# Key and value projection of axis 1: its second token tile moved right behind the first, in the PSUM bank of the group statistics

## The chip, the core and the metric

The kernel is one program on 1 core of a Trainium2 chip. The metric is the time of one execution on the device in microseconds (us), less is better. TensorE (PE) multiplies into PSUM; VectorE (DVE), ScalarE (ACT) and GpSimd (POOL) do the elementwise work; SyncE (SP) issues most transfers. Each engine takes its own instructions in order, and the engines meet at semaphores that the kernel sets and waits for by hand.

## What is computed

The input x is 8 images of 16 x 16 tokens with 256 channels. Two blocks follow each other, each with a residual:

```python
x = x + L0(_gn(x))      # linear attention: 16 heads of 16 channels, once along the columns, once along the rows
x = x + L1(_gn(x))      # softmax attention along rows and along columns, 256 channels, Gaussian distance term

# L0, for one axis (sequences of 16 tokens):
q, k, v = split(x @ w_qkv)
dots = einsum('bhie,bhje->bhij', q, k) * d ** (-0.5)
out = einsum('bhij,bhje->bhie', dots, v) @ w_out     # the two axes are added
# L1:
r_attn = softmax(q @ k over w - gw * dist);  c_attn = softmax(q @ k over h - gw * dist)
out = (r_attn @ v + c_attn @ v) @ Wo + bo
```

`_gn` is a group normalisation over 32 groups of 8 channels and all 256 tokens of an image. L0 has no softmax, so the kernel forms key-times-value first and multiplies the queries into it.

## The kernel before

One image is one batch step b, 0 to 7. Its 256 tokens are two token tiles of 128, its 256 channels two channel halves. Nearly every product runs as three passes (hi times hi, hi times lo, lo times hi) over operands that are split in two FP32R parts: ScalarE writes the high part from PSUM, VectorE writes the low part as the difference. All these products stand on line 995 in the helper `product`.

The order of work is written out by hand for each engine, as `attention(b)` and then `project(b)`, unrolled for b = 0, in a loop for b = 1 to 6, and with a tail of its own for b = 7. Each step works on three images at once: L0's attention of image b, L1's softmax attention of image b-1, and L0's projections of image b+1.

What matters here, by name:

- `project_kv(b+1, i)` on TensorE makes keys and values (512 columns) of tile i of the next image: i = 0 and 1 are the two token tiles of axis 1, i = 2 and 3 those of axis 0. It is 6 matmuls of 128x512 into `proj_bank[i]`. `take_kv(b+1, i)` on ScalarE (L383) copies the bank to SBUF and raises `kv_taken`.
- `place_v` on SyncE waits until both tiles of an axis are taken and issues 8 transfers (L253) that lay the values out by sequence in `v_wide`. `key_value(b+1, axis)` on TensorE (L1050) waits for them.
- `project_q(b+1, 0)` (12 matmuls of 128x256) makes the queries of axis 1, and `take_q` (L387) copies them.
- L0's output of image b: `transpose_output(b, axis)` on TensorE (L1081), `split_o(b, axis)` on ScalarE (L409, the high part `o_hi`) and on VectorE (L676, the low part `o_lo`), then `project_out(b, axis)` on TensorE (12 matmuls). Axis 1 goes first.
- L1's weights of image b-1: `exponentials` on ScalarE (L415, L417), `invert_sums` on VectorE (L715), `weights` on GpSimd (L342 to L348), then `transpose_weights` on TensorE (L1127).
- `group_mean` (L1000) and `group_variance` (L1004) average the statistics over a group in columns 0 to 3 of `bank[1]`, for both normalisations. `normalise(1, b)` on ScalarE (L375) follows from them, and after it `mask_kv` (L394) and the next step's `queries` (L1072).

TensorE's order around the change is: `transpose_output(b, 1)`, `project_kv(b+1, 0)`, `project_q(b+1, 0)`, `transpose_output(b, 0)`, `project_out(b, 1)`, `project_kv(b+1, 1)`, `project_out(b, 0)`, then in `project` `project_kv(b+1, 2)`, `transpose_weights(b-1)`, `project_kv(b+1, 3)`, `group_mean(1, b)`. ScalarE's order is: `split_o(b, 1)`, `take_kv(0)`, `take_q(0)`, `split_o(b, 0)`, `exponentials`, `take_kv(1)`, `take_kv(2)`. Tile 1 goes to `bank[2]`, which the transposed output of axis 1 holds until `o_lo` has been read.

```python
def project(b, has_prev, has_next):
    if has_next:
        take_kv(b + 1, 1)
        take_kv(b + 1, 2)
```

Of the kernel before, what the change touches and what calls it, by code (L numbers as in the profile page):

```python
# [23 lines left out]
TILES = 2 * TT  # L24
# [11 lines left out]
def tile_of(n):  # L36

    return 1 - n // TT, n % TT


def build(nc, x, w_qkv0, w_out0, w_qkv1, w_out1, wq, bq, wk, bk, wv, bv, wo, bo, sigma, out):
    with ExitStack() as ctx:
# [3 lines left out]
        def sem(name):  # L46
            return ctx.enter_context(nc.semaphore(name))
# [88 lines left out]
        bank = [ctx.enter_context(nc.psum_tensor(f"bank{i}", [P, 512], FP32)) for i in range(8)]  # L136
# [6 lines left out]
        last_s_bank, last_at_bank, last_pv_bank = [bank[3], bank[0]], [bank[2], bank[6]], [bank[1], bank[4]]  # L143
        o_last = o_even[:, :, :, :].rearrange("p h m a -> p (h m a)").rearrange("p (c n) -> p c n", c=CC)
        t_last, vp_last, at_last, y_last, x1b_last = x_in, x_res, q[:, 0, :, :], q[:, 1, :, :], k_v[:, 0, 0, :, :]
        proj_bank, q_bank = [bank[0], bank[2], bank[4], bank[5]], [bank[7], bank[7]]
        first_bank = [bank[0], bank[3]]
        fold_bank, values_fold_bank = bank[7], bank[0]
        xt_first = attn
# [29 lines left out]
        kv_proj, kv_taken = sem("kv_proj"), sem("kv_taken")  # L179
# [181 lines left out]
        def _(act):  # L361
# [17 lines left out]
            def take_kv(b, i):  # L379
                axis, t = tile_of(i)  # L380
                src = proj_bank[i]
                act.wait_ge(kv_proj, TILES * b + i + 1)
                act.activation(k_v[:, axis, t, :, :].rearrange("p i d -> p (i d)"), src[:, :], ACT.Copy).then_inc(kv_taken, 1)  # L383

            def take_q(b, i, scale=1.0):
                act.wait_ge(q_proj, 2 * b + i + 1)
                act.activation(q[:, 1 - i, :, :].rearrange("p c n -> p (c n)"), q_bank[i][:, :], ACT.Copy, scale=scale).then_inc(q_taken, 1)  # L387
# [11 lines left out]
            def take_even(b, axis):  # L399

                act.wait_ge(o_ready, 2 * b + 2 - axis)
                for r in range(HALVES):
                    src = qkv_bank[r][:, :].rearrange("p (m s a) -> p m s a", m=TT * CC, s=2)
                    act.activation(o_even[:, r, :, :], src[:, :, 0, :], ACT.Copy, scale=parity[:, 0:1]).then_inc(o_even_done, 1)  # L404
# [19 lines left out]
            def high_t(b):  # L424
                act.wait_ge(t_ready, b + 1)
                for c in range(CC):
                    last = act.activation(t_hi[:, c, :], t_bank[:, c * TOKENS:(c + 1) * TOKENS], ACT.Identity, bias=c1[:, c:c + 1])
                last.then_inc(t_hi_done, 1)

            def high_values(b, t):  # L430
                act.wait_ge(vp_ready, TT * b + t + 1)
                act.activation(vp_hi[:, t, :], vp_banks[t][:, 0:DIM], ACT.Copy).then_inc(vp_hi_done, 1)

            def attention(b, has_prev, has_next):
                take_even(b, 1)
                if has_prev:
                    high_t(b - 1)
                mask_kv(b, 0)
                if has_prev:
                    high_values(b - 1, 0)  # L440
                if has_next:
                    normalise(0, b + 1)
                if has_prev:
                    high_values(b - 1, 1)
                take_even(b, 0)
                split_o(b, 1)
                if has_next:
                    take_kv(b + 1, 0)
                    take_q(b + 1, 0)
                split_o(b, 0)  # L450
                if has_prev:
                    exponentials(b - 1, 0)
                    exponentials(b - 1, 1)

            def next_residual(b):

                act.wait_ge(x1_ready, b)
                act.wait_ge(x_turned, b)
                act.dma_start(x_res[:, :, :], x_chan[:, :, :]).then_inc(res_loaded, 16)

            def project(b, has_prev, has_next):
                if has_next:
                    take_kv(b + 1, 1)
                    take_kv(b + 1, 2)
                    next_residual(b + 1)
                if has_prev:
                    split_attn(b - 1)
                if has_next:
                    take_kv(b + 1, 3)
                if not has_prev:  # L470
                    high_fold(wvo_hi, 3, values_fold_bank)
                normalise(1, b)
                if has_next:
                    mask_kv(b + 1, 1)
                    take_q(b + 1, 1)
# [512 lines left out]
        def _(pe):  # L988
# [9 lines left out]
            def group_mean(k, b):  # L998
                pe.wait_ge(stat_in[k], 2 * b + 1)
                pe.matmul(stat_bank[:, 0:CC], group_avg[:, :], mv[k][:, :, 0], start=True, stop=True).then_inc(stat_sum[k], 1)  # L1000
# [10 lines left out]
            def project_kv(b, i):  # L1011

                axis, t = tile_of(i)
                if i == 0:
                    pe.wait_ge(xn_split[0], b)
                if i == TT:
                    pe.wait_ge(turned, b + 1)
                hi, lo = (xt_hi, xt_lo) if axis == 0 else (xn_hi[0], xn_lo[0])
                product(proj_bank[i][:, :],
                        [((hi[:, c, t * P:(t + 1) * P], lo[:, c, t * P:(t + 1) * P]),  # L1020
                          (wqkv_hi[:, axis, c, DIM:3 * DIM], wqkv_lo[:, axis, c, DIM:3 * DIM])) for c in range(CC)]
                        ).then_inc(kv_proj, 1)
# [156 lines left out]
            def attention(b, has_prev, has_next):  # L1179

                queries(b, 1)
                if has_prev:
                    pe.wait_ge(q_taken, 2 * (b + 1))
                    project_t(b - 1)
                if has_next:
                    group_mean(0, b + 1)
                key_value(b, 0)
                if has_next:
                    group_variance(0, b + 1)
                if has_prev:  # L1190
                    project_values(b - 1, 0)
                    project_values(b - 1, 1)
                else:
                    fold_row()
                queries(b, 0)
                if has_prev:
                    pe.wait_ge(vp_lo_done, TT * (b - 1) + 1)
                    scores(b - 1, 0, y_bank)
                    scores(b - 1, 1, y_bank)
                transpose_output(b, 1)  # L1200
                if has_next:
                    if not has_prev:
                        pe.wait_ge(w_split, 1)
                    project_kv(b + 1, 0)
                    if has_prev:
                        pe.wait_ge(vp_lo_done, TT * b)
                    else:
                        pe.wait_ge(bias_step, 5)
                    project_q(b + 1, 0)
                transpose_output(b, 0)  # L1210
                if has_prev:
                    pe.wait_ge(logits_done, TT * b)
                else:
                    pe.wait_ge(w_split, 3)
                    pe.wait_ge(fold_split, 1)
                project_out(b, 1)
                if has_next:
                    project_kv(b + 1, 1)
                project_out(b, 0)

            def project(b, has_prev, has_next):

                if has_next:
                    project_kv(b + 1, 2)
                if has_prev:
                    if has_next:
                        pe.wait_ge(q_taken, 2 * (b + 1) + 1)
                    transpose_weights(b - 1)
                if has_next:
                    project_kv(b + 1, 3)  # L1230
                group_mean(1, b)
                if has_prev:
                    weighted_values(b - 1, 0)
                else:
                    fold_values(0)
                group_variance(1, b)
                if has_prev:
                    weighted_values(b - 1, 1)
                else:
                    fold_values(1)  # L1240
                if has_next:
                    key_value(b + 1, 1)
                    if has_prev:
                        pe.wait_ge(out_sum, b)
                    else:
                        pe.wait_ge(q_taken, 2 * (b + 1) + 1)
                    project_q(b + 1, 1)
                if not has_prev:
                    pe.wait_ge(fold_split, 2)
                    pe.wait_ge(r_split, 2)  # L1250
# [76 lines left out]
            fold_row()  # L1327
            pe.wait_ge(w_split, 1)
            project_kv(1, 0)
            pe.wait_ge(bias_step, 5)  # L1330
            project_q(1, 0)
            transpose_output(0, 0)
            pe.wait_ge(w_split, 3)
            pe.wait_ge(fold_split, 1)
            project_out(0, 1)
            project_kv(1, 1)
            project_out(0, 0)
            project(0, False, True)
            with pe.Fori(1, BATCHES - 1) as b:
# [113 lines left out]
```

## Time and profile before

| what | value |
|---|---|
| time, median of 3 runs | 244.22 us (243.4 to 245.59) |
| the profiled execution, its own time | 244.0 us |
| its span, first to last instruction | 242.2 us |
| mean granted TensorE clock | 0.971 of full speed |
| TensorE busy | 224.0 us, 92% of the span |
| VectorE busy | 172.0 us, 71% |
| ScalarE busy | 131.5 us, 54% |
| GpSimd busy | 67.2 us, 28% |
| transfers | 13.86 MB, mean 57 GB/s |

One loop step takes about 25.7 us. Batch b stands for the step that works on L0's attention of image b: batch 3 runs from about 102.9 to 128.6 us of the span. In a timeline row the first number is the start from the beginning of the span, the second the length; the brackets at its end give the idle time of the engine before it and what ended that. Matmuls overlap each other, so the distance from start to start says what one costs, not its length.

### The profile page before, as it was taken

The page shows a single profiled execution, that of the slowest core. Times are in us where ns is not written, and L with a number is a line of the kernel's source. Part 1 is how long each engine was busy: PE and PEld are TensorE (multiplying, and loading weights), DVE is VectorE, ACT ScalarE, POOL GpSimd, SP SyncE. Part 2 cuts the span into 40 slices and gives each one's busy share as a digit, 9 for nine tenths or more (in the row PEclk, how much of TensorE's full clock was granted, in tenths as well). Part 3 has the DMA queues.
Part 4 walks back from the last instruction along what each step waited for, and adds up shares of the span by engine and source line. Part 5 has one row for each costly group of instructions (what it writes and reads, how often), then busy time and mean ns, then how long its engine had stood idle before and what let it go on. Part 6 is the DMA issues. An engine that isn't in the chain of part 4 may idle for free.

```text
span 242.2 us, 8272 instructions
## 1 busy us (share of the span) xinstructions
PE 224.0 (92%) x3216; PEld 192.6 (80%) x3216; DVE 172.0 (71%) x507; ACT 131.5 (54%) x321; POOL 67.2 (28%) x94
## 2 busy tenths in 40 slices
PE   7999999889998999999999999999999999993980
PEld 7747889688986898789888897889878988792960
DVE  5769666687757885788568866888588856687480
ACT  2435743367736665565656673777366656726240
POOL 6400160203432164216420543124421642002000
PEclk9999979999999999999999999999999999997696
DMA  6932230322021321332032203221220212011003
GB/s 215 344 55 67 52 55 6 95 46 38 0 80 46 53 43 32 83 58 43 10 93 55 43 16 92 51 43 30 81 49 0 43 56 65 14 27 19 0 3 87
DMA packets 43824, 13.86 MB, mean 57 GB/s; under 512 B 36257, under 2 KB 42401, under 8 KB 43809
## 3 DMA queue, kind: packets, MB, share of 16 engines
q1 hardware_dynamic: 41264, 9.92, 19.8%
q10 hardware_dynamic: 2544, 3.74, 4.4%
q8 instruction: 10, 0.16, 0.3%
q14 instruction: 6, 0.04, 0.1%
HBM read 5.51 MB, written 2.10 MB: 31 GB/s over the span
## 4 chain that ended last, share of the span: by engine, by line
PE 69%; SPq 9%; ACT 5%; issue 5%; DMA 4%; DVE 3%; ACTq 2%; POOL 1%; POOLq 0%; DVEq 0%
PE bank L995 39%; SPq L253 9%; PE bank L1072 8%; PE bank L1050 6%; DMA v_wide<-k_v 4%; PE bank L1081 3%; PE bank L1256 3%; ACT k_v L383 2%; PE bank L1270 1%; PE bank L1004 1%; ACTq L499 1%; ACT kv L394 1%; PE bank L1009 1%; PE bank L1424 1%; PE bank L1174 1%
## 5 line engine op out<-in xcount | busy, mean ns | idle before, releaser
L383 ACT ACTIVATE k_v<-bank 128x512 f32<-128x512 f32 x32 | 19.0, 598 | 35.4 <-PE bank L995 29.7
L308 POOL TENSOR_TENSOR rstd<-var_eps,minus_half 128x2 f32<-128x2 f32 x16 | 11.3, 705 | 92.1 <-DVE var_eps L640 92.1
L394 ACT ACTIVATE kv<-bank,head_scale 128x256 f32<-128x256 f32 x64 | 25.0, 472 | 4.6 <-PE bank L1050 4.6
L299 POOL TENSOR_TENSOR xt_lo<-xn,xn_hi 128x256 fp32r<-128x256 f32 x14 | 18.5, 1341 | 20.9 <-DVE xn_hi L649 20.9
L657 DVE TENSOR_TENSOR kv<-bank,block_mask 128x512 f32<-128x512 f32 x32 | 20.6, 684 | 3.8 <-PE bank L1050 3.8
L1072 PE MATMUL bank<-kv,q 64*32 64x128 f32 x1024 | 19.2, 281 | 3.7 <-issue 2.3
L1050 PE MATMUL bank<-v_wide,k_v 64*32 64x128 f32 x1024 | 18.4, 273 | 2.2 <-DMA v_wide<-k_v 1.0
L1072 PEld LDWEIGHTS bank<-kv,q 64*32 64x32 f32 x1024 | 15.2, 108 | 6.5 <-issue 6.5
L404 ACT ACTIVATE o_even<-bank,parity 128x256 f32<-128x256 f32 x32 | 13.3, 469 | 8.6 <-PE bank L1072 8.6
L1050 PEld LDWEIGHTS bank<-v_wide,k_v 64*32 64x32 f32 x1024 | 14.4, 105 | 4.3 <-issue 4.0
L995 PE MATMUL bank<-o_hi,wout_hi 128*128 128x256 f32 x60 | 17.5, 292 | 0.0
L676 DVE TENSOR_TENSOR o_lo<-bank,o_hi 128x256 fp32r<-128x256 f32 x30 | 13.8, 505 | 4.7 <-ACT o_hi L409 4.7
L668 DVE SCALAR_TENSOR_TENSOR o_tok<-bank,parity,o_even 128x256 f32<-128x256 f32 x32 | 14.0, 478 | 4.6 <-ACT o_even L404 4.6
L995 PE MATMUL bank<-o_hi,wout_lo 128*128 128x256 f32 x60 | 17.0, 284 | 0.0
L995 PE MATMUL bank<-o_lo,wout_hi 128*128 128x256 f32 x60 | 16.9, 282 | 0.0
L409 ACT ACTIVATE o_hi<-bank 128x256 fp32r<-128x256 f32 x30 | 12.7, 505 | 3.0 <-PE bank L1081 3.0
L375 ACT ACTIVATE xn<-x,nbias,rstd 128x256 f32<-128x256 f32 x14 | 7.7, 594 | 11.9 <-DVE nbias L645 11.9
L387 ACT ACTIVATE q<-bank 128x512 f32<-128x512 f32 x16 | 9.6, 598 | 7.9 <-PE bank L995 5.9
L342 POOL TENSOR_TENSOR attn<-exp_col,inv_sum 128x512 f32<-128x512 f32 x6 | 6.3, 1042 | 20.5 <-DVE inv_sum L715 20.5
L771 DVE TENSOR_TENSOR x<-bank,x_res 128x512 f32<-128x512 f32 x7 | 4.8, 692 | 9.9 <-PE bank L995 9.9
L995 PE MATMUL bank<-wqkv_hi,xn_hi 128*128 128x512 f32 x28 | 11.7, 418 | 0.0
L995 PEld LDWEIGHTS bank<-o_hi,wout_hi 128*128 128x128 f32 x60 | 11.3, 189 | 0.3
(233 smaller groups left out, 698.5 us busy)
## 6 DMA issues: line engine op xcount, KB each, us to landing
v_wide<-k_v SPq DMA_DIRECT2D x122, 32.0 KB, 2.0
x_blk<-in_x_dram SPq DMA_DIRECT2D x56, 32.0 KB, 1.9
x_res<-x_chan ACTq DMA_DIRECT2D x7, 256.0 KB, 2.3
out_dram<-y_blk SPq DMA_DIRECT2D x56, 32.0 KB, 1.5
wqkv_in<-in_L_conv_w_qkv_dram SPq DMA_DIRECT2D x2, 384.0 KB, 6.4
wqkv_in<-in_L_conv_w_qkv_dram ACTq DMA_DIRECT2D x2, 384.0 KB, 7.6
wl<-in_L_conv_Wq_dram SPq DMA_DIRECT2D x1, 256.0 KB, 3.5
wl<-in_L_conv_Wk_dram ACTq DMA_DIRECT2D x1, 256.0 KB, 3.9
```

The costliest lines, as they stand in the source:

```text
L253: sp.dma_start(v_wide[tokens, axis, :, s % NEAR, :], k_v[tokens, axis, :, 1, :]).then_inc(v_placed[axis], 16)
L299: pool.tensor_tensor(xt_lo[:, c, :].rearrange("p (w h) -> p w h", w=SIDE), by_axis(xn[0][:, c, :], 0), by_axis(xn_hi[0][:, c, :].bitcast(F ...
L383: act.activation(k_v[:, axis, t, :, :].rearrange("p i d -> p (i d)"), src[:, :], ACT.Copy).then_inc(kv_taken, 1)
L394: last = act.activation(kv[axis][:, 1, :, :, :, head // 2, own].rearrange("p t c s e -> p (t c s) e"), kv_bank[1][:, :].rearrange("p (a e) ...
L404: act.activation(o_even[:, r, :, :], src[:, :, 0, :], ACT.Copy, scale=parity[:, 0:1]).then_inc(o_even_done, 1)
L409: last = act.activation(by_axis(o_hi[:, axis, c, :], axis), banks[1 - axis][:, c * TOKENS:(c + 1) * TOKENS].rearrange("p (s i) -> p s i", ...
L657: last = dve.tensor_tensor(kv[axis][:, 0, :, :, :, pair, :].rearrange("p t c s e -> p (t c s) e"), kv_bank[0][:, :].rearrange("p (a e) -> ...
L668: last = dve.scalar_tensor_tensor(o_tok[:, axis, :, :].rearrange("p t (c h a) -> p (t c) h a", c=CC, h=HALVES)[:, :, r, :], src[:, :, 1, : ...
L676: last = dve.tensor_tensor(by_axis(o_lo[:, axis, c, :], axis), banks[1 - axis][:, c * TOKENS:(c + 1) * TOKENS].rearrange("p (s i) -> p s i ...
L995: last = pe.matmul(dst, a, b, start=(first and i == 0), stop=(final and i == len(passes) - 1))
L1050: last = pe.matmul(kv_bank[r][pair * PAIR:(pair + 1) * PAIR, first:first + P], k_v[rows, axis, t, 0, channels], v_wide[rows, axis, t, :, c ...
L1072: last = pe.matmul(qkv_bank[r][quad * QUAD:(quad + 1) * QUAD, to:to + 2 * FOUR], q[rows, axis, c, first:first + QUAD], kv[axis][rows, quad ...
```

## The change

The second tile of axis 1, `project_kv(b+1, 1)`, moves on TensorE from between the two `project_out` of an image to right behind `project_kv(b+1, 0)`, for b+1 = 1 to 7. ScalarE's `take_kv(b+1, 1)` moves with it, from behind the exponentials to right behind `take_kv(b+1, 0)`. The tile's bank is `bank[1]` instead of `bank[2]`. Since `group_mean(1, b)` writes into `bank[1]` too, TensorE now waits before it until tile 1 has been taken. The first image uses the same table of banks, its order is unchanged.

```diff
-        proj_bank, q_bank = [bank[0], bank[2], bank[4], bank[5]], [bank[7], bank[7]]
+        proj_bank, q_bank = [bank[0], bank[1], bank[4], bank[5]], [bank[7], bank[7]]
...
                 split_o(b, 1)
                 if has_next:
                     take_kv(b + 1, 0)
+                    take_kv(b + 1, 1)
                     take_q(b + 1, 0)
                 split_o(b, 0)
...
             def project(b, has_prev, has_next):
                 if has_next:
-                    take_kv(b + 1, 1)
                     take_kv(b + 1, 2)
...
                     project_kv(b + 1, 0)
+                    project_kv(b + 1, 1)
                     if has_prev:
                         pe.wait_ge(vp_lo_done, TT * b)
...
                 project_out(b, 1)
-                if has_next:
-                    project_kv(b + 1, 1)
                 project_out(b, 0)
...
                 if has_next:
                     project_kv(b + 1, 3)
+                    pe.wait_ge(kv_taken, TILES * (b + 1) + 2)
                 group_mean(1, b)
...
             project_kv(1, 0)
+            project_kv(1, 1)
...
             project_out(0, 1)
-            project_kv(1, 1)
             project_out(0, 0)
```

On TensorE, in the loop step, the stretch from the last pass of `project_out(b, 1)` stands like this before (`wqkv` rows are the key and value projection, `wout` rows the output projection, `o_lo_done` says that VectorE has written the low part):

```order
L995 MATMUL bank<-o_hi,wout_lo 128x256
L995 MATMUL bank<-wqkv_hi,xn_hi 128x512
L995 MATMUL bank<-wqkv_lo,xn_hi 128x512
L995 MATMUL bank<-wqkv_hi,xn_lo 128x512
L995 MATMUL bank<-wqkv_hi,xn_hi 128x512
L995 MATMUL bank<-wqkv_lo,xn_hi 128x512
L995 MATMUL bank<-wqkv_hi,xn_lo 128x512
L995 MATMUL bank<-o_hi,wout_hi 128x256 [waits o_lo_done]
```

The six passes of the projection stand between the two output projections. After the change the same place on TensorE, from the middle of `project_out(b, 1)`, reads:

```order
L995 MATMUL bank<-o_hi,wout_hi 128x256
L995 MATMUL bank<-o_lo,wout_hi 128x256
L995 MATMUL bank<-o_hi,wout_lo 128x256
L995 MATMUL bank<-o_hi,wout_hi 128x256 [waits o_lo_done]
L995 MATMUL bank<-o_lo,wout_hi 128x256
L995 MATMUL bank<-o_hi,wout_lo 128x256
```

The row that waits for `o_lo_done` now comes right behind the last pass of `project_out(b, 1)`; the six passes stand ahead of the queries' projection.

On ScalarE, in the loop step, the row order from the axis-1 split to the next image's tiles is before (`o_hi` the high part of the output, 128x16x16 that of axis 0; `k_v` the taken keys and values):

```order
L409 ACTIVATE o_hi<-bank 128x256
L382 ISA
L383 ACTIVATE k_v<-bank 128x512 [waits kv_proj]
L386 ISA
L387 ACTIVATE q<-bank 128x512 [waits q_proj]
L409 ACTIVATE o_hi<-bank 128x16x16 [waits ot_ready]
L409 ACTIVATE o_hi<-bank 128x16x16
L415 ACTIVATE exp_row,exp_sum<-log_row,neg_max 128x128 [waits max_ready]
L417 ACTIVATE exp_col,exp_sum<-log_col,neg_max 128x256
L415 ACTIVATE exp_row,exp_sum<-log_row,neg_max 128x128 [waits max_ready]
L417 ACTIVATE exp_col,exp_sum<-log_col,neg_max 128x256
L382 REGISTER_ALU
```

After it, the same place of ScalarE reads:

```order
L409 ACTIVATE o_hi<-bank 128x256
L382 ISA
L383 ACTIVATE k_v<-bank 128x512 [waits kv_proj]
L382 REGISTER_ALU
L383 ACTIVATE k_v<-bank 128x512 [waits kv_proj]
L386 ISA
L387 ACTIVATE q<-bank 128x512 [waits q_proj]
L409 ACTIVATE o_hi<-bank 128x16x16 [waits ot_ready]
L409 ACTIVATE o_hi<-bank 128x16x16
L415 ACTIVATE exp_row,exp_sum<-log_row,neg_max 128x128 [waits max_ready]
L417 ACTIVATE exp_col,exp_sum<-log_col,neg_max 128x256
```

The second `k_v` row has moved ahead of the queries, of the axis-0 split and of the exponentials. VectorE's and GpSimd's orders are the same in both kernels.

## Rows read from the trace of the kernel before

**Rows 1.** The page: busy share of each engine, and the chain's shares by engine

```profile
PE 224.0 (92%) x3216; PEld 192.6 (80%) x3216; DVE 172.0 (71%) x507; ACT 131.5 (54%) x321; POOL 67.2 (28%) x94
...
PE 69%; SPq 9%; ACT 5%; issue 5%; DMA 4%; DVE 3%; ACTq 2%; POOL 1%; POOLq 0%; DVEq 0%
```

**Rows 2.** Chain of work that ended last, batch 3: start us, us, engine line

```profile
118.26 0.61 ACT k_v L383
118.88 0.61 SPq L253
...
123.36 1.99 DMA v_wide<-k_v
```

**Rows 3.** Waits of TensorE over the span: us in total, times, longest

```profile
PE bank L1050 <- DMA v_wide<-k_v: 1.0, 3, 0.7
```

**Rows 4.** Timeline of TensorE, batch 3: start us, us, engine line op tiles [idle before]

```profile
116.66 0.40 PE L995 MATMUL bank<-wqkv_hi,xn_hi 128*128 128x512 f32 x1
...
118.06 0.28 PE L995 MATMUL bank<-o_hi,wout_hi 128*128 128x256 f32 x1
...
120.66 0.40 PE L995 MATMUL bank<-wqkv_hi,xt_lo 128*128 128x512 f32 x1
121.11 0.63 PE L1127 MATMUL bank<-ident,attn 128*128 128x128 f32 x4
```

**Rows 5.** Timeline of ScalarE, the same stretch

```profile
114.98 0.60 ACT L387 ACTIVATE q<-bank 128x512 f32<-128x512 f32 x1 [0.84 <-PE bank L995]
115.47 1.06 ACT L409 ACTIVATE o_hi<-bank 128x256 fp32r<-128x256 f32 x2
116.32 0.38 ACT L415 ACTIVATE exp_row<-log_row,neg_max 128x128 f32<-128x128 f32 x1
...
117.95 0.20 ACT L417 ACTIVATION_READ_ACCUMULATOR exp_col<-log_col,neg_max 128x1 f32 x1
```

**Rows 6.** Timeline of VectorE, the same stretch

```profile
116.56 1.13 DVE L676 TENSOR_TENSOR o_lo<-bank,o_hi 128x256 fp32r<-128x256 f32 x2 [0.65 <-ACT o_hi L409]
118.18 0.18 DVE L715 RECIPROCAL inv_sum<-exp_sum 128x4 f32<-128x4 f32 x1 [0.49 <-ACT exp_col L417]
```

**Rows 7.** Timeline of GpSimd, the same stretch

```profile
120.13 0.88 POOL L348 TENSOR_TENSOR attn<-row_weights,attn 128x128 f32<-128x128 f32 x2
```

**Rows 8.** Timeline of TensorE, the end of batch 3

```profile
124.08 0.38 PE L1004 MATMUL bank<-shift,group_avg 128*128 128x2 f32 x2
...
125.49 1.15 PE L1050 MATMUL bank<-v_wide,k_v 64*32 64x128 f32 x64 [0.20 <-DMA v_wide<-k_v]
...
128.56 1.15 PE L1072 MATMUL bank<-kv,q 64*32 64x128 f32 x64 [0.31 <-issue]
```

**Rows 9.** Timeline of ScalarE, the end of batch 3

```profile
125.68 1.09 ACT L375 ACTIVATE xn<-x,nbias,rstd 128x256 f32<-128x256 f32 x2 [1.91 <-DVE nbias L645]
126.69 1.57 ACT L394 ACTIVATE kv<-bank,head_scale 128x256 f32<-128x256 f32 x4
```

**Rows 10.** Timeline of TensorE, the end of batch 1

```profile
72.08 0.38 PE L1004 MATMUL bank<-shift,group_avg 128*128 128x2 f32 x2
...
73.96 1.15 PE L1050 MATMUL bank<-v_wide,k_v 64*32 64x128 f32 x64 [0.68 <-DMA v_wide<-k_v]
...
77.13 1.13 PE L1072 MATMUL bank<-kv,q 64*32 64x128 f32 x63 [0.40 <-issue]
```

**Rows 11.** Timeline of VectorE, batch 0

```profile
38.70 1.11 DVE L676 TENSOR_TENSOR o_lo<-bank,o_hi 128x256 fp32r<-128x256 f32 x2 [0.81 <-ACT o_hi L409]
```

**Rows 12.** Timeline of TensorE, batch 0

```profile
40.09 0.28 PE L995 MATMUL bank<-o_hi,wout_hi 128*128 128x256 f32 x1
```

**Rows 13.** Stretches: A:B, length, busy us of each engine, granted clock, DMA share, GB/s

```profile
30.00:33.00 3.00, 3.00 (x70) 2.62 (x71) 1.66 (x4) 1.70 (x5) 1.55 (x2) 0.51 0.33 54
...
210.00:220.00 10.00, 7.96 (x113) 6.96 (x112) 8.59 (x26) 5.18 (x17) 1.04 (x1) 1.00 0.16 28
220.00:228.00 8.00, 5.83 (x27) 5.29 (x27) 4.26 (x15) 2.88 (x6) 0.74 (x1) 0.58 0.00 0
```

## The prediction

> **What bounds the kernel now.** I read the page first. TensorE is busy for 92% of the span and holds 69% of the chain that ended last; SyncE's queue and the transfers hold 13% more [rows 1]. So either more work or more waiting on TensorE shows in the time, unless it falls where TensorE already waits.
>
> Then the chain in order of time. In batch 3 it leaves TensorE at the copy of tile 1 (118.26 us), runs through SyncE's 8 issues of `v_wide` and the landing of the last (123.36 + 1.99 = 125.35), and comes back into TensorE at `key_value(b+1, 1)` [rows 2], which sat idle for 0.20 us for it [rows 8]. This is where an earlier tile 1 could help. The list of waits says how little TensorE pays there: 1.0 us in three waits over the whole span [rows 3].
>
> Last I read the stretch around the moved tile on all four engines. Two chains run beside TensorE there, and both start when `project_q(b+1, 0)` ends, because ScalarE takes the queries first and everything else behind them:
> - queries taken at 114.98, `o_hi` of axis 0 from 115.47 to 116.53 [rows 5], `o_lo` from 116.56 to 117.69 [rows 6], then TensorE may start `project_out(b, 0)`. It did so at 118.06 [rows 4]: 0.37 us of slack.
> - the exponentials from 116.32, the last sum read out at 118.15 [rows 5], the reciprocal at 118.18 [rows 6], GpSimd's weights ready at 120.13 + 0.88 = 121.01 [rows 7], then `transpose_weights` at 121.11 [rows 4]. This chain has no slack. The last pass of the projection ahead of it started at 120.66, and such passes follow each other by 0.23 us ((118.06 - 116.66) / 6), so TensorE could have gone on at 120.89. It already waited 0.22 us for GpSimd, and started 0.10 us after the weights were ready.
>
> **What the change does to these chains.** The tile costs 118.06 - 116.66 = 1.40 us on TensorE [rows 4]. No work is added: the same 1.40 us are now spent before `project_q(b+1, 0)` instead of behind it. Both chains start at the end of `project_q`, so both start 1.40 us later, while the TensorE work that covers them, between the end of `project_q` and each waiting instruction, is 1.40 us shorter.
>
> *First wait, `project_out(b, 0)`.* ScalarE takes tile 1 in the 1.40 us in which TensorE makes the queries, and was idle for 0.84 us there [rows 5]; the copy of 0.61 us [rows 2] fits. So `take_q` starts at 114.98 + 1.40 = 116.38, `o_hi` ends at 117.93, `o_lo` at 117.69 + 1.40 = 119.09. VectorE has nothing else then: it was idle for 0.65 us before [rows 6]. TensorE, with its earlier work unchanged in sum, would be ready at 118.06. It starts at 119.09 plus about 0.1 for the semaphore (the 0.10 of the weights, above): about 119.2, a stall of 1.1 us. Queued behind it are `project_kv(b+1, 2)` and all the rest of the step, and VectorE's residual `x1` waits for it.
>
> *Second wait, `transpose_weights(b-1)`.* The weights are ready at 121.01 + 1.40 = 122.41, and TensorE can start at 122.51. From the first stall alone TensorE would be ready at 120.89 + 1.1 = 122.0. So the second wait tops the first up to the full 1.40 us: the two do not add. Since this chain had no slack before, the step becomes longer by 1.40 us behind it, whatever the first wait does.
>
> *The end of the step.* What the change frees is the idle time for `v_wide`: tile 1 is taken at about 114.94 to 115.54 instead of 118.26 to 118.87, 3.3 us earlier, so its transfers land long before `key_value(b+1, 1)`. In a common step that buys nothing. From `group_variance(1, b)` at 124.08 two paths run to the next step's queries at 128.56 [rows 8]: TensorE's own, and VectorE, GpSimd and ScalarE with `normalise(1, b)` from 125.68 and the masking of the keys and values from 126.69 to 128.26 [rows 9]. ScalarE goes from the one to the other without a pause, so an earlier `key_value` does not make the masking earlier. Gain 0 in the five steps 2 to 6. Batch 1 is the exception: `key_value` waited 0.68 us and the queries came 77.13 - 72.08 = 5.05 us after `group_variance` [rows 10], against 128.56 - 124.08 = 4.48 in batch 3 [rows 8]. That step gets 5.05 - 4.48 = 0.57, say 0.6 us back.
>
> *Batch 0* has no exponentials and no weights. Its `o_lo` ends at 38.70 + 1.11 = 39.81 [rows 11] and `project_out(0, 0)` started at 40.09 [rows 12]. With 1.40 later: 41.21 + 0.1 = 41.3, a stall of 1.2 us, and nothing behind it takes that back. Batch 7 projects no next image and has no stall of its own.
>
> *Edits that I cost at nothing.* The new wait for `kv_taken` before `group_mean(1, b)`: the copy ends near 115.5, and the mean comes behind two more projections of the step. Without this cover TensorE would wait for a copy of 0.6 us. The transfers of axis 0 now wait for the copy of tile 3 instead of following those of axis 1 on SyncE's queue; that copy moves with TensorE and is over before 124.08, and 8 issues and a landing take 125.35 - 118.88 = 6.5 us [rows 2], so until 130.6. `key_value(b+1, 0)` stands behind the next queries (128.56 + 1.15, [rows 8]) and 12 passes of 256 columns, each half of 0.23: 131.1. Close, but covered, and both ends move together. The new bank: TensorE writes it only after VectorE has read the statistics of the first normalisation, which lie a whole attention stretch back.
>
> *The sum:* batch 0 +1.2, batches 1 to 6 6 x 1.40 = +8.4, batch 1 -0.6: +9.0 us. On the profiled execution's own 244.0 us (span 242.2) that makes 253.0 us; on the median of the runs, 244.22, it would be 253.2, which is no difference.
>
> *Bounds.* The least I can make of the stalls is that GpSimd's chain somehow tightens by 0.3 us per step and only the first wait counts: 1.2 + 6 x 1.1 - 0.6 = 7.2. The most, without the gain in batch 1 and with 0.1 us more per step: 1.2 + 9.0 = 10.2. On top comes the tail. TensorE's clock fell there after a stretch with 7.96 us of work in 10, and ran at 0.58 of full speed on the mean from 220 to 228 us [rows 13]. That costs up to 0.42 x 5.8 = 2.4 us, and where exactly the clock falls may shift now that the tail comes 9 us later: about 1 us either way. So 250.5 to 255.5.
>
> *The clock in the loop.* What the rows show: the granted clock held 1.00 over a stretch with 2.04 us idle in 10, and it fell to 0.51, which is the lower level of 1.2 GHz, from 30 to 33 us, and to 0.58 on the mean from 220 to 228 [rows 13]. In the new step TensorE is idle for 1.4 us within some 5 us. By the Trainium skill, page "TensorE: Matmul & The Clock Gate", section "The HAM clock gate", the chip watches how busy TensorE has been and halves its clock after an idle stretch; that rule speaks against this change, since it would multiply a small stall. The trace bears it out for the tail, where the clock fell behind the stretch with the 2.04 us of idle time, and does not rule it out for the loop. By the rule the time would be that of rival 2, without it the sum above stands.
>
> **The rivals.**
> 1. *The transfer wait was the real bound, and the stalls don't come* (not slower). For it: 13% of the chain lies on SyncE and transfers. It would give back the 1.0 us of waits on `v_wide` [rows 3] and some 0.5 us in batch 0: 242.5 us. It decides if `o_lo` and the weights are ready within the shortened cover, that is if both chains could run 1.40 us ahead. Against it: both hang on the end of `project_q` through ScalarE's order, with 0.37 and 0 us of slack.
> 2. *The stalls pull the clock down.* Once per loop step a stretch as from 30 to 33 us, at 0.51: 3.0 x 0.49 = 1.5 us lost, 6 times, +9 on top: 262 us. Against it: 1.4 us of idle time is split in two parts, and 7.96 busy in 10 us was still granted 1.00 [rows 13].
> 3. *Only the first wait costs*, because the weights' chain has hidden slack: 244.0 + 7.2 = 251.2 us. Against it: in batch 3 the transposes start 0.10 us after the weights, on time for no other reason.
>
> **How the numbers follow.** The forecast (both chains, 253.0) gets 0.82, rival 3 0.06, rival 2 0.06, rival 1 0.06. The predicted time is the forecast's. The range 250.5 to 255.5 holds the forecast with its bounds and rival 3, and leaves out rivals 1 and 2. One per cent is 2.4 us, about what a measurement of this kernel tells from no change. The forecast and rivals 2 and 3 are slower by more than that, 0.94. Rival 1 at 242.5 is 0.7% below; I give 0.04 to within 1% and 0.02 to faster.
>
> **What would show it.** In the profile after, TensorE should sit idle about 1.1 us before the second output projection, in each step from batch 0 to 6, with VectorE's `o_lo` as the releaser; about 0.5 us before `transpose_weights` behind GpSimd; a loop step should take some 27.1 us instead of 25.7; `key_value(b+1, 1)` should wait for no transfer; and the chain that ended last should run through ScalarE's `o_hi` and exponentials and GpSimd instead of SyncE. I am wrong if a loop step keeps its 25.7 us, if the granted clock in the loop falls below 1.00, or if `project_out(b, 0)` starts less than 0.5 us later than its cover allows.

## The result and the profile after

| | before | after |
|---|---|---|
| time, median | 243.81 us (242.09 to 245.59, 4 runs) | 252.87 us (251.73 to 254.9, 4 runs) |
| ratio to before | | 1.038, 95% interval 1.027 to 1.049 |
| profiled execution, its own time | 244.0 us | 251.89 us |
| its span | 242.2 us | 250.1 us |
| TensorE busy | 224.0 us | 223.3 us |
| mean granted clock | 0.971 | 0.967 |

The ratios here and in the table of experiments leave out runs more than 1.5% above the fastest of the same kernel; since the runs of one kernel spread by 3% and more, that can leave 7 of 19 runs of one kernel beside all 10 of another, and a ratio can differ from that of the medians by over 1%.

The change makes the kernel slower by about 9 us. TensorE does the same work in the same time; the span is longer by waiting. The page of the kernel after, the row of busy shares and the chain's shares by engine, answers to [rows 1]:

```profile
PE 223.3 (89%) x3216; PEld 191.4 (77%) x3216; DVE 171.6 (69%) x507; ACT 130.7 (52%) x321; POOL 67.1 (27%) x94
...
PE 70%; issue 9%; DVE 8%; ACT 7%; POOL 2%; POOLq 0%; DVEq 0%
```

SyncE and the transfers have left the chain altogether (they held 13%), and VectorE, ScalarE and GpSimd hold 17% where they held 9%. The bottleneck that the change aimed at is gone from the chain, and two others have come into it. The list of TensorE's waits over the span names them (total, times, longest; `issue` is a wait that the profile puts down to nobody):

```profile
PE bank L995 <- DVE o_lo L676: 6.4, 7, 1.0
...
PE bank L1127 <- issue: 1.9, 6, 0.3
```

The first of the two is new: seven waits for `o_lo`, one in each batch from 0 to 6. The wait for `v_wide` of [rows 3] is no longer in the list.

The timelines of batch 3 show both chains. TensorE, against [rows 4]: the last pass of `project_out(b, 1)`, the first of `project_out(b, 0)`, the last pass ahead of the weights' transposes, and these.

```profile
119.53 0.28 PE L995 MATMUL bank<-o_hi,wout_lo 128*128 128x256 f32 x1
120.73 0.39 PE L995 MATMUL bank<-o_hi,wout_hi 128*128 128x256 f32 x1 [0.93 <-DVE o_lo L676]
...
123.42 0.40 PE L995 MATMUL bank<-wqkv_hi,xt_lo 128*128 128x512 f32 x1
124.11 0.63 PE L1127 MATMUL bank<-ident,attn 128*128 128x128 f32 x4 [0.29 <-issue]
```

The passes of `project_out` follow each other by 0.12 us, so TensorE was ready at 119.65 and started at 120.73: 1.08 us lost. After the pass at 123.42 it was ready at 123.65 and started the transposes at 124.11: 0.46 us. ScalarE, against [rows 5], now with the copy of tile 1 ahead of the queries:

```profile
116.57 0.60 ACT L383 ACTIVATE k_v<-bank 128x512 f32<-128x512 f32 x1 [0.80 <-PE bank L995]
118.00 0.60 ACT L387 ACTIVATE q<-bank 128x512 f32<-128x512 f32 x1 [0.82 <-PE bank L995]
118.49 1.06 ACT L409 ACTIVATE o_hi<-bank 128x256 fp32r<-128x256 f32 x2
119.33 0.37 ACT L415 ACTIVATE exp_row<-log_row,neg_max 128x128 f32<-128x128 f32 x1
...
120.96 0.20 ACT L417 ACTIVATION_READ_ACCUMULATOR exp_col<-log_col,neg_max 128x1 f32 x1
```

The queries' copy starts at 118.00 and releases all the rest: `o_hi`, then the exponentials, as before, 1.4 us later in the step. VectorE and GpSimd, against [rows 6] and [rows 7]:

```profile
119.58 1.09 DVE L676 TENSOR_TENSOR o_lo<-bank,o_hi 128x256 fp32r<-128x256 f32 x2 [2.04 <-ACT o_hi L409]
121.19 0.18 DVE L715 RECIPROCAL inv_sum<-exp_sum 128x4 f32<-128x4 f32 x1 [0.51 <-ACT exp_col L417]
```

```profile
123.14 0.87 POOL L348 TENSOR_TENSOR attn<-row_weights,attn 128x128 f32<-128x128 f32 x2
```

`o_lo` ends at 120.67 and TensorE goes on at 120.73; the weights are ready at 124.01 and the transposes start at 124.11, 0.10 us behind them as before. The chain that ended last, in order of time, tells the same in one piece:

```profile
118.00 0.51 ACT q L387
118.50 1.06 ACT o_hi L409 x2
119.58 1.11 DVE o_lo L676 x2
120.73 3.08 PE bank L995 x18
123.82 0.29 issue
124.11 0.63 PE bank L1127 x4
```

Before, it ran in this place from the copy of tile 1 through eight issues of SyncE [rows 2]. At the step's end, against [rows 8]:

```profile
127.08 0.38 PE L1004 MATMUL bank<-shift,group_avg 128*128 128x2 f32 x2
...
128.22 1.16 PE L1050 MATMUL bank<-v_wide,k_v 64*32 64x128 f32 x64
...
131.52 1.15 PE L1072 MATMUL bank<-kv,q 64*32 64x128 f32 x64 [0.53 <-issue]
```

`key_value` waits for no transfer, and 131.52 - 127.08 = 4.44 us lie between the variance and the next queries, where 4.48 did.

**A measure that the clock leaves alone.** The start of `queries(b, 1)` marks a step. TensorE's clock does not fall between the first loop step and the last in these two kernels, so the distance from batch 1's queries to batch 7's, six steps, compares the loops alone. Before:

```profile
50.75 1.15 PE L1072 MATMUL bank<-kv,q 64*32 64x128 f32 x64 [0.58 <-issue]
...
205.27 1.15 PE L1072 MATMUL bank<-kv,q 64*32 64x128 f32 x64
```

After:

```profile
50.44 1.15 PE L1072 MATMUL bank<-kv,q 64*32 64x128 f32 x64 [1.20 <-DVE kv L657]
...
212.41 1.15 PE L1072 MATMUL bank<-kv,q 64*32 64x128 f32 x64 [0.28 <-ACT kv L394]
```

That is 154.52 us against 161.97: +7.45. By steps, before: 26.38, 25.73, 25.70, 25.63, 25.64, 25.44. After: 27.04, 27.03, 27.01, 27.03, 27.03, 26.83. Ahead of it, batch 0 from the first pass of `project_kv(1, 0)` (33.92 and 32.46 us) to batch 1's queries took 50.75 - 33.92 = 16.83 us and takes 50.44 - 32.46 = 17.98: +1.15. So the change costs 7.45 + 1.15 = 8.60 us; TensorE's granted clock reads 1.00 over all of these stretches, in both kernels. The two spans differ by 7.9 us only: the head up to that pass was 1.46 us shorter and the tail behind batch 7's queries 0.76 us longer (-1.46 + 8.60 + 0.76 = 7.9). The order of the work is the same there in both kernels; what is known of the head is in the section on the hardware.

### The profile page after: what moved, and what is told of

Its sections match the earlier page's. It is cut to its first block, busy times and chain, and to the rows that moved or that the text cites. A ratio compares the mean times of both kernels' runs of the same rounds, so it can differ in the third digit from the quotient of the medians.

```text
span 250.1 us, 8279 instructions
## 1 busy us (share of the span) xinstructions
PE 223.3 (89%) x3216; PEld 191.4 (77%) x3216; DVE 171.6 (69%) x507; ACT 130.7 (52%) x321; POOL 67.1 (27%) x94
## 4 chain that ended last, share of the span: by engine, by line
PE 70%; issue 9%; DVE 8%; ACT 7%; POOL 2%; POOLq 0%; DVEq 0%
PE bank L995 42%; PE bank L1072 6%; PE bank L1050 6%; PE bank L1256 4%; DVE o_lo L676 3%; ACT o_hi L409 3%; PE bank L1004 2%; PE bank L1127 2%; DVE kv L657 1%; ACT q L387 1%; ACT kv L394 1%; PE bank L1270 1%; PE bank L1081 1%; PE bank L1398 1%; POOL xt_lo L299 1%
## 5 line engine op out<-in xcount | busy, mean ns | idle before, releaser
L995 PE MATMUL bank<-o_hi,wout_hi 128*128 128x256 f32 x60 | 18.3, 306 | 6.4 <-DVE o_lo L676 6.4
L995 PE MATMUL bank<-wqkv_hi,xt_hi 128*128 128x512 f32 x28 | 11.5, 410 | 0.0
```

What stands on the lines that cost most here:

```text
L995: last = pe.matmul(dst, a, b, start=(first and i == 0), stop=(final and i == len(passes) - 1))
```

## The experiments

Each kernel was compared with the kernel before on the same chip. "Six steps" is the distance from above, from each one's profiled execution; the medians are over all runs. For what the loop costs, go by the six steps: they have 154.52, 154.54 and 154.47 us for the kernel before, e1 and e8, whose medians range over 2 us.

| kernel | median, us | before, us | ratio (95% interval) | six steps, us |
|---|---|---|---|---|
| the change | 252.87 | 243.81 | 1.038 (1.027 to 1.049) | 161.97 |
| e1 bank and wait alone | 242.23 | 243.86 | 1.000 (0.992 to 1.008) | 154.54 |
| e2 tile 1 behind the transposes | 242.52 | 243.86 | 1.000 (0.992 to 1.007) | 154.24 |
| e3 tile 2 as cover | 252.55 | 243.86 | 1.045 (1.034 to 1.055) | 161.91 |
| e4 tile 3 ahead too | 254.64 | 243.86 | 1.049 (1.037 to 1.061) | 163.81 |
| e6 chains off the queries | 246.03 | 243.90 | 1.011 (1.004 to 1.018) | 153.47 |
| e7 and the mean ahead | 244.13 | 243.90 | 1.008 (1.003 to 1.013) | 152.13 |
| e8 mean ahead, tile 1 in its old place | 244.41 | 243.90 | 0.986 (0.981 to 0.992) | 154.47 |
| e9 e7 with the old batch 0 | 242.31 | 242.49 | 0.994 (0.989 to 1.000) | 152.89 |
| e10 the change with the old batch 0 | 250.83 | 242.49 | 1.035 (1.029 to 1.041) | 162.27 |

**e1: the bank and the wait alone.** The kernel before with two edits, every instruction in its place:

```diff
-        proj_bank, q_bank = [bank[0], bank[2], bank[4], bank[5]], [bank[7], bank[7]]
+        proj_bank, q_bank = [bank[0], bank[1], bank[4], bank[5]], [bank[7], bank[7]]
...
                     project_kv(b + 1, 3)
+                    pe.wait_ge(kv_taken, TILES * (b + 1) + 2)
                 group_mean(1, b)
```

> The kernel before, with tile 1 in bank[1] and the new wait of TensorE ahead of the group mean, but every instruction in its old place. Theory (the place of the tile costs, because it takes the cover from two chains): no difference to before, ratio 1.00 within 0.005, a loop step of 25.7 us, no idle time before the group mean. Rival (the shared bank or the added wait costs): slower than before by a part of the 9 us, with idle time of TensorE before the group mean behind ScalarE's copy.

Six steps of 154.54 against 154.52. Sharing the bank of the statistics and the new wait cost nothing; the whole cost is in the order.

**e2: tile 1 earlier, but behind the transposes.** e1, with the tile moved between `transpose_output(b, 0)` and `project_out(b, 1)`:

```diff
                 transpose_output(b, 0)
+                if has_next:
+                    project_kv(b + 1, 1)
...
                 project_out(b, 1)
-                if has_next:
-                    project_kv(b + 1, 1)
                 project_out(b, 0)
```

> Bank[1] as in the change, tile 1 on TensorE earlier than before, but behind the queries' projection and the axis-0 transposes and ahead of both output projections; ScalarE takes it where it did before. Theory: both chains start as early as before and have all their cover, so a loop step of 25.7 us, ratio to before 1.00 within 0.005, no idle time before the second output projection. Rival (tile 1 anywhere ahead of the output projection costs, for instance because the axis-1 projection is delayed): near the changed kernel, 253 us, step 27.0.

```profile
50.00 1.15 PE L1072 MATMUL bank<-kv,q 64*32 64x128 f32 x64 [1.20 <-DVE kv L657]
...
75.79 1.15 PE L1072 MATMUL bank<-kv,q 64*32 64x128 f32 x64 [0.31 <-issue]
```

The loop is as fast as before. The tile may stand ahead of both output projections, so long as it stands behind the point at which the two chains start. These two rows show batch 1's step: 25.79 us instead of 26.38. That is not all gain: `key_value` still waited 0.31 us for `v_wide` in it (0.68 before), another wait of 0.32 us for `v_wide` came right behind it, and batch 2 took 26.03 us instead of 25.73; the six steps together are 0.28 us shorter.

**e3: tile 2 as cover for the first wait.** The changed kernel, with

```diff
                 project_out(b, 1)
+                if has_next:
+                    project_kv(b + 1, 2)
                 project_out(b, 0)
...
-                if has_next:
-                    project_kv(b + 1, 2)
                 if has_prev:
                     if has_next:
                         pe.wait_ge(q_taken, 2 * (b + 1) + 1)
```

> The changed kernel with tile 2 (axis 0) moved up on TensorE between the two output projections, where tile 1 stood before. That gives the o_lo chain its cover back and leaves the weights' chain with the same total cover as in the changed kernel. Theory (two waits that overlap, the weights' chain sets the step): the idle 0.9 us before the second output projection goes, the idle time before the weights' transposes grows from 0.3 to about 1.3 us, the step stays at 27.0 us, ratio to before 1.035. Rival 3 of the prediction (only the o_lo wait costs): a step of 26.0 us, ratio about 1.01.

The wait for `o_lo` is gone from TensorE's list, and the one before the weights' transposes has grown from 1.9 us in all to

```profile
PE bank L1127 <- issue: 8.8, 6, 1.5
```

```profile
103.86 1.15 PE L1072 MATMUL bank<-kv,q 64*32 64x128 f32 x64 [0.53 <-issue]
...
123.47 0.63 PE L1127 MATMUL bank<-ident,attn 128*128 128x128 f32 x4 [1.48 <-issue]
...
130.92 1.15 PE L1072 MATMUL bank<-kv,q 64*32 64x128 f32 x64 [0.57 <-issue]
```

The step is 130.92 - 103.86 = 27.06 us. Taking away the larger of the two waits (1.08 us, against 0.46) gave nothing, because the weights' chain sets the step. This settles that the two waits overlap and do not add, and that rival 3 was wrong.

**e4: tile 3 ahead of the weights' transposes too.** e3, with

```diff
+                if has_next:
+                    project_kv(b + 1, 3)
                 if has_prev:
...
                     transpose_weights(b - 1)
                 if has_next:
-                    project_kv(b + 1, 3)
                     pe.wait_ge(kv_taken, TILES * (b + 1) + 2)
```

and on ScalarE `take_kv(b + 1, 3)` ahead of `split_attn(b - 1)`.

> As e3, with tile 3 moved ahead of the weights' transposes too, on TensorE and in ScalarE's copies. Theory: the wait for the weights goes (1.4 us more cover), but the transposes cannot start earlier than the weights are ready, and high and low part of the transposed weights have lost the cover of tile 3: the idle time moves to the first weighted value, about 1.2 us behind VectorE's at_lo; the step stays near 27.0 us, ratio 1.03 to 1.04. Rival (cover for the weights' transposes is all that is missing): a step of 25.8, ratio 1.00 to 1.01.

```profile
PE bank L995 <- DVE at_lo L697: 6.7, 6, 1.2
```

```profile
127.52 0.63 PE L1127 MATMUL bank<-ident,attn 128*128 128x128 f32 x4
128.17 0.35 PE L1000 MATMUL bank<-mv,group_avg 128*128 128x2 f32 x2
129.56 0.39 PE L995 MATMUL bank<-at_hi,vp_hi 128*128 128x256 f32 x1 [1.03 <-DVE at_lo L697]
```

The wait has moved one station on, as expected: the transposes are on time, and the first weighted value waits for `at_lo`. Steps of 26.81 us alternate with steps of 27.8 us, which was not expected; the clock fell in the longer ones (the section on the hardware), so that the six steps of 163.81 hold that too. Tile 3 was as much a cover for the next chain as tile 1 was for these two.

**e6: both chains freed from the queries' projection.** The changed kernel; on TensorE `transpose_output(b, 0)` goes ahead of `project_q(b+1, 0)`, on ScalarE

```diff
                     take_kv(b + 1, 1)
-                    take_q(b + 1, 0)
                 split_o(b, 0)
                 if has_prev:
                     exponentials(b - 1, 0)
                     exponentials(b - 1, 1)
+                if has_next:
+                    take_q(b + 1, 0)
```

> The changed kernel, tile 1 in its new place and bank, with the start of both chains freed from the queries' projection: the axis-0 transposes on TensorE ahead of project_q, and on ScalarE the axis-0 split and the exponentials ahead of take_q. Theory (the 1.4 us come only from both chains hanging on the end of project_q): both waits go, the step is 25.6 us, batch 1 keeps its 0.6 us gain, ratio to before 0.995 to 1.00. Rival (tile 1 ahead of the output projection is itself the cost, or the copy on ScalarE): a step of 27 us, ratio 1.035.

```profile
102.34 1.15 PE L1073 MATMUL bank<-kv,q 64*32 64x128 f32 x64 [0.52 <-issue]
...
120.54 0.63 PE L1128 MATMUL bank<-ident,attn 128*128 128x128 f32 x4
...
127.94 1.15 PE L1073 MATMUL bank<-kv,q 64*32 64x128 f32 x64 [0.53 <-issue]
```

A step of 127.94 - 102.34 = 25.60 us, with tile 1 exactly where the change puts it. This is the strongest evidence for the mechanism: not the place of the tile costs, but that the two chains started behind it. Six steps take 1.05 us less than before, 0.75 of it in batch 1 (25.63 instead of 26.38). The ratio was expected at 0.995 to 1.00 and came out as 1.011, from 4 runs; the loop is not the reason (see the head in the section on the hardware).

**e7: and the group mean ahead of tile 3.** e6, with

```diff
+                if has_prev:
...
+                    group_mean(1, b)
                 if has_next:
                     project_kv(b + 1, 3)
+                if has_prev:
+                    group_variance(1, b)
+                    weighted_values(b - 1, 0)
```

and on VectorE `spread(1, b)` ahead of `split_attn(b - 1)`.

> As e6, and the group mean of the second normalisation moved ahead of tile 3, the group variance right behind tile 3, on VectorE the spread ahead of at_lo. Theory: the path from the variance to the next queries (4.44 us) starts about 0.9 us earlier, values of axis 1 are in place already, so the step falls by 0.7 to 0.8 us to about 24.9, ratio to before 0.975 to 0.985. Rival (TensorE's own work fills the step): no gain over e6, 25.6.

```profile
122.90 0.63 PE L1128 MATMUL bank<-ident,attn 128*128 128x128 f32 x4
...
126.99 1.16 PE L1051 MATMUL bank<-v_wide,k_v 64*32 64x128 f32 x64
...
130.07 1.15 PE L1073 MATMUL bank<-kv,q 64*32 64x128 f32 x64 [0.31 <-issue]
```

```profile
128.20 1.57 ACT L394 ACTIVATE kv<-bank,head_scale 128x256 f32<-128x256 f32 x4 [0.37 <-PE bank L1051]
```

The common step is 25.4 us (for one, 130.07 - 104.69 = 25.38), 0.2 us less than e6 and not 0.7. The expectation was wrong in size: with the variance early, ScalarE's masking no longer follows its normalisation without a pause. It waits 0.37 us for `key_value` (the last row), which starts 3.08 us before the queries. The ratio of 1.008, with a loop 2.39 us shorter than before, comes from outside the loop: batch 1's queries started at 53.74 us in this execution and at 50.75 in that of the kernel before.

**e8: the mean ahead, tile 1 in its old place.** The kernel before with e7's move of the mean alone.

> The kernel before with only the move of the group mean and variance of e7; tile 1 in its old place and bank, taken late. Theory: now the transfer of the values of axis 1 is what the step ends on: key_value waits for it some 0.5 to 0.7 us in each loop step, and the step falls only by 0.2 to 0.3 us to 25.4, ratio 0.99 to 1.00. Rival (the early values of tile 1 are worth nothing, the mean alone gives the gain): 24.9 as in e7.

```profile
PE bank L1050 <- DMA v_wide<-k_v: 2.7, 7, 0.9
```

```profile
123.02 0.63 PE L1127 MATMUL bank<-ident,attn 128*128 128x128 f32 x4
...
127.37 1.15 PE L1050 MATMUL bank<-v_wide,k_v 64*32 64x128 f32 x64 [0.28 <-DMA v_wide<-k_v]
...
130.49 0.80 PE L1072 MATMUL bank<-kv,q 64*32 64x128 f32 x39 [0.36 <-issue]
```

TensorE now waits for the transfers in seven places, 2.7 us in all, and six steps take 154.47 us: the mean's move gives nothing at all, where 0.2 to 0.3 us per step were expected. The wait in a common step was 0.24 to 0.39 us, less than the 0.5 to 0.7 expected. From the transposes to `key_value` it takes 4.35 us here and 4.09 in e7. So the early tile is worth 0.26 us per step, but only where the chains are freed and the variance is early. Its ratio of 0.986 does not come from the loop: it rests on 4 of its 11 runs, three of them with a mean clock of 0.99, and the medians are 244.41 and 243.90.

**e9 and e10: batch 0 as in the kernel before.** e7 and the changed kernel, with `project_kv(1, 1)` of the unrolled batch 0 back between its two output projections and its transposes and copies in the old order.

> e7 with batch 0 in the order of the kernel before, so that only the loop differs. The stretch from the first to the seventh start of the axis-1 queries should be 2 us shorter than before (154.5), as in e7, since the steps of 25.4 stay. Theory A (the head's low clock in e6 and e7 follows from the changed order of batch 0): the head ends as early as in the kernel before on the mean, and the time is 2 us below it, ratio 0.985 to 0.992. Theory B (where the clock falls in the head is chance): some runs keep a mean clock of 0.98 to 0.99 as the kernel before has, some do not, the interval is wide, and the ratio lies anywhere from 0.985 to 1.005.

> The changed kernel with batch 0 in the order of the kernel before; the loop as changed. Theory: batch 0's stall of 1.1 us goes, the six loop steps stay at 27.0 us, first to seventh start of the queries 162 us, ratio to before about 1.030 to 1.035. Rival (batch 0 carries more than its own 1.1 us): ratio under 1.025.

e10 keeps its six steps (162.27) and 1.035 of the time: the loop carries the cost. The ratios of 1.038 and 1.035, each good to about 0.01, are too coarse to size batch 0's share; the two traces above give it as 1.15 us. e9's loop is 1.63 us shorter than before, one step less good than e7's by a wait of 0.8 us for a transfer, and its ratio is 0.994 with an interval that ends at 1.000: theory B's range holds it, theory A's does not. It is the best candidate to beat both kernels, by about half a per cent; the measurement does not settle it.

## Why the prediction was right

Predicted: 253.0 us, +9.0; measured: 252.87 us as the median, 251.89 in the profiled execution, and a cost of 8.60 us in the two traces over stretches at full clock. The mechanism was right. That the median came within 0.13 us is luck: the four runs spread over 3.2 us. The range held rival 3 as well (251.2), so the time alone does not tell the two apart; e3 does.

- *Both chains start at the end of `project_q`* [rows 5]. Right, and shown by e6 and e2: start them earlier, or put the tile behind their start, and the cost is gone.
- *First wait, 1.1 us.* Right: 1.08 in batch 3, `o_lo` as the releaser in all seven batches.
- *Second wait tops it up to 1.40.* Right in kind: 0.46 us before the transposes, which include the 0.22 that stood there already, and e3 shows that this wait alone sets the step. In size, the steps of batches 2 and 3 grew by 1.30 and 1.31, the later ones by 1.39 to 1.40: 6.8 us where 5 x 1.40 = 7.0 stood. Batches 2 and 3 are those in which `key_value` had waited for a transfer before (0.16 and 0.20 us), so the gain that the working put at nothing there may be these 0.09 us; that is not shown, since e1 has waits of 0.17 to 0.20 us in steps of 25.66.
- *Batch 1, +1.40 less 0.6.* That is +0.8; measured +0.66 (27.04 against 26.38). The working named the reason rightly: the transfers' wait of 0.68 us [rows 10] went, and in the steps where ScalarE's masking follows its normalisation without a pause [rows 9] nothing came back.
- *Batch 0, +1.2.* Measured +1.15.
- *The added wait and the shared bank at nothing.* Right, e1.
- *Rival 1*, the transfers as the real bound: they did leave the chain, and it gained nothing outside batch 1. e7 against e8 shows what the early tile is worth once other things are moved: 0.26 us per step.
- *Rival 2*, the clock: it held 1.00 through the loop of the changed kernel, so the rival failed here. But e4 has it fall in a loop of nearly the same idle time, in every other step and for 1.0 us each, where the rival priced 1.5 us in each step. The chance of 0.06 looks low for the kind, and the price was high.
- *The tail's clock within about 1 us*: +0.76 behind batch 7's queries; the clock fell about 16.0 us behind them before and 17.5 us after, and how much of the 0.76 that makes was not traced. What the working left out is the head. It allowed for a spread only in the tail, while the head moved by 1.46 us between the two profiles, and batch 1's queries start anywhere from 47.35 us (e9) to 53.74 us (e7) among the experiments, of which about 1.2 us is batch 0's own stall. The sum had no term for that.

## What to carry to other kernels

Before work is moved up on a busy engine, ask which chains on other engines start behind its new place, and how much work still stands between their start and the instruction that waits for them: the moved piece is lost from that cover in full, even if its own consumer gains. Where two such waits follow each other, the later one with no slack sets the cost; covering the first alone gives nothing. Work can be moved if the producers that others wait for are put ahead of it, on the engine that makes them and on those that copy them.

## What the runs showed of the hardware

**The head decides more between executions than most edits.** TensorE's granted clock from 26 to 42 us of the span (columns: stretch, length, busy us of TensorE, weight load, VectorE, ScalarE, GpSimd, clock, DMA share, GB/s), in the kernel before, in e1 and in e7:

```profile
26.00:42.00 16.00, 15.70 (x217) 14.42 (x217) 10.50 (x29) 7.64 (x18) 4.38 (x5) 0.89 0.23 37
```

```profile
26.00:42.00 16.00, 15.71 (x197) 14.02 (x182) 11.49 (x30) 7.87 (x17) 5.50 (x5) 1.00 0.25 52
```

```profile
26.00:42.00 16.00, 15.70 (x192) 13.75 (x192) 8.74 (x26) 7.15 (x18) 4.36 (x5) 0.68 0.24 39
```

The instructions ahead of 30 us are of the same kinds and order in all three; TensorE is busy for 15.7 us each time. The lower level is 0.5, which is 1.2 GHz. The kernel before spent 3.4 us at it there, e8 6.8, e10 10.2, e1 none. From batch 0's queries to batch 1's, with batch 0's work in the old order in all four, they took 26.30, 27.88, 29.14 and 25.04 us: 3.4 us at the lower level cost 1.3 us, 6.8 cost 2.8 and 10.2 cost 4.1. e7 spent 10.2 us at it too.

That is one part only. Batch 1's queries start at 50.75 us in the kernel before and at 47.59 in e1, 3.16 us apart, and 1.90 us of it is there at batch 0's queries already (24.45 and 22.55). The same holds for the 1.46 us between the kernel before and the changed one: from 26 to 42 us both have a mean clock of 0.89. Of the 1.46 us, 1.32 are there ahead of 12 us, and 0.86 of these come from eight equal passes that went at different speeds. Here they are with the passes behind them, first in the kernel before, then in the changed one:

```profile
7.63 3.76 PE L1270 MATMUL bank<-wl 128*128 128x256 f32 x8
11.18 4.51 PE L1256 MATMUL bank<-wqkv_in,xn 128*128 128x512 f32 x8
```

```profile
7.17 2.89 PE L1270 MATMUL bank<-wl 128*128 128x256 f32 x8
9.86 4.41 PE L1256 MATMUL bank<-wqkv_in,xn 128*128 128x512 f32 x8
```

The eight passes take 3.55 and 2.69 us from their start to the next row's; in e1 they were over in 1.97. The granted clock in the profile does not account for it: over these passes it reads 1.00 in the kernel before and in e1, and 0.67 on the mean in the changed kernel, which went through them faster than the kernel before. The cause of this part stays open.

The runs of the kernel before spread from 239.9 to 247.4 us, and the mean clock goes with the time, if not in strict order: those at 239.9 to 240.1 us had 0.983 or more, the slowest 0.957. In the 14 runs of e6 and e7 the mean clock never came above 0.965; with the old batch 0, in e9, four of 12 runs had 0.978 or 0.979. This could be an influence of batch 0's order on how long the clock stays low, but it is not shown: the runs are few, the profiled executions of e8 and e10 have the old batch 0 and long stays at the lower level, and what in that stretch the chip reacts to was not tried.

**In the loop, too, the clock can fall or hold over the same work.** Two stretches of e4 from the weights' transposes to the next queries, batches 2 and 3:

```profile
99.70:107.90 8.20, 7.04 (x96) 5.97 (x97) 5.25 (x17) 3.92 (x9) 1.74 (x2) 0.79 0.26 72
127.50:134.70 7.20, 5.60 (x96) 4.80 (x97) 5.42 (x17) 4.03 (x9) 1.74 (x2) 1.00 0.24 73
```

They do the same work, 96 instructions of TensorE each; in the first the clock fell, to 0.79 on the mean, and the step took 27.84 us, in the second it held 1.00 and the step took 26.81. Ahead of the fall TensorE had waited 1.05 us for `at_lo`, and in the second stretch it waited 1.03 us at the same place. e3 has longer single waits, 1.46 to 1.48 us, and kept the full clock over its step:

```profile
103.90:130.90 27.00, 24.84 (x396) 22.12 (x397) 19.32 (x57) 15.44 (x40) 8.76 (x11) 1.00 0.23 49
```

So neither the longest wait nor the idle time of a step (27.00 - 24.84 = 2.16 us there) tells by itself whether the clock falls. In the profiled execution of the changed kernel the clock held 1.00 through the loop.
